# An early-fusion embedding kernel: GpSimd's products of the graph edges go to VectorE, with four node numbers packed in a register

## The reference, cut to what matters

```python
def _gat(x, src, dst, W, a_s, a_d, bias):
    h = (x @ W).reshape(G, Jn, H, C)
    es = jnp.einsum('gjhc,hc->gjh', h, a_s)[:, src]
    ed = jnp.einsum('gjhc,hc->gjh', h, a_d)[:, dst]
    e = jax.nn.leaky_relu(es + ed, 0.2)
    ...
    w = jnp.exp(e - m[:, dst])
    den = jnp.zeros((G, Jn, H), e.dtype).at[:, dst].add(w)
    alpha = w / den[:, dst]
    out = jnp.zeros((G, Jn, H, C), e.dtype).at[:, dst].add(alpha[..., None] * h[:, src])
    return out.reshape(G, Jn, H * C) + bias
```

## Time and profile before

| what | us |
|---|---|
| device time, median of 3 runs (lowest to highest) | 6471.19 (6469.46 to 6471.34) |
| the profiled execution | 6495.84 |
| its span | 6494.1 |
| VectorE busy in the span | 5697.2 |
| GpSimd busy | 4760.5 |
| TensorE busy (matmuls) | 3920.4 |
| ScalarE busy | 3243.8 |

### The profile page before, as it was taken

How to read it: one execution, slowest core, us unless ns; L and a number is a source line. 1 busy time by engine, 2 the same in 40 slices (tenths; PEclk the granted TensorE clock), 3 DMA queues, 4 the chain that set the end, 5 groups by cost and what they waited for, 6 DMA issues and landing times. The chain is left out here.

```text
span 6494.1 us, 61166 instructions
## 1 busy us (share of the span) xinstructions
PE 3920.4 (60%) x13720; PEld 2254.6 (35%) x13720; DVE 5697.2 (88%) x7312; ACT 3243.8 (50%) x5534; POOL 4760.5 (73%) x3337
## 2 busy tenths in 40 slices
PE   3213412215676776776767767767667676667777
PEld 3102411213343333333433333334333333245556
DVE  3677666765999999999999999999999999967778
ACT  1112211214566656666666666666566665544445
POOL 4362145225999999999999999999999999833334
PEclk9656556657999999999999999999999999987878
DMA  1000000003444444444444444444444444300000
GB/s 26 1 1 11 2 1 1 11 18 116 160 163 168 160 166 165 160 174 160 165 165 160 166 164 161 173 160 165 165 160 166 164 160 170 141 4 2 2 2 2
DMA packets 171496, 695.04 MB, mean 107 GB/s; under 512 B 27970, under 2 KB 34627, under 8 KB 171139
## 3 DMA queue, kind: packets, MB, share of 16 engines
q1 hardware_dynamic: 169608, 688.25, 29.6%
q0 software_dynamic: 1536, 3.14, 0.2%
HBM read 684.77 MB, written 6.55 MB: 106 GB/s over the span
## 5 line engine op out<-in xcount | busy, mean ns | idle before, releaser
L1022 PE MATMUL m_PS<-m_pr,ident 128*128 128x512 f32 (+1 forms) x6144 | 2496.3, 544 | 907.3 <-DVE m_pr L1146 907.1
L806 POOL TENSOR_TENSOR m_hs<-m_u,m_BC 128x1280 f32<-128x1280 f32 x1024 | 2975.9, 2906 | 68.6 <-DVE m_u L1163 68.6
L1138 DVE TENSOR_TENSOR_SCAN m_hs<-m_PS,m_hs 128x640 f32<-128x640 f32 x2048 | 2934.8, 1467 | 5.2 <-POOL m_hs L806 3.0
L863 ACT ACTIVATE m_PS<-m_dt,m_A 128x640 f32<-128x640 f32 x2048 | 1613.3, 794 | 909.9 <-DVE m_hs L1138 896.3
L1022 PEld LDWEIGHTS m_PS<-m_pr,ident 128*128 128x128 f32 x6144 | 1134.9, 195 | 2167.8 <-DVE m_pr L1146 1133.1
L813 POOL TENSOR_TENSOR m_pr<-m_hs,m_BC 128x384 f32<-128x384 f32 x1024 | 1070.1, 1045 | 184.5 <-DVE m_hs L1138 179.9
L1146 DVE TENSOR_TENSOR m_pr<-m_hs,m_PS 128x896 f32<-128x896 f32 x1024 | 1079.8, 1055 | 8.2 <-DVE m_hs L1138 8.0
L270 POOL TENSOR_TENSOR g_prod<-g_hbuf,g_E 128x128 f32<-128x128 f32 (+1 forms) x888 | 471.1, 548 | 832.7 <-ACT g_E L320 636.3
L852 ACT COPY m_PS<-m_BC 128x448 f32<-128x448 f32 x1024 | 546.5, 534 | 155.8 <-DVE m_pr L1146 107.5
L354 PE MATMUL g_TB<-ident,g_nrm 128*128 128x128 f32 x200 | 66.2, 332 | 574.7 <-DVE g_nrm L490 569.9
L557 DVE TENSOR_TENSOR g_accA<-g_accA,g_prod 128x128 f32 x592 | 255.2, 431 | 158.0 <-DVE g_accA L557 122.1
(11 more groups left out here) (241 smaller groups left out, 4435.8 us busy)
## 6 DMA issues: line engine op xcount, KB each, us to landing
m_BC<-m_scr SPq DMA_DIRECT2D x1024, 640.0 KB, 3.8
m_scr<-m_CB SPq DMA_DIRECT2D x32, 160.0 KB, 4.2
m_hs<-in_cwr SPq DMA_DIRECT2D x4, 512.0 KB, 3.9
out<-f_res SPq DMA_DIRECT2D x20, 64.0 KB, 1.5
m_inw<-in_in_w SPq DMA_DIRECT2D x4, 256.0 KB, 4.0
m_dtw<-in_dw SPq DMA_DIRECT2D x4, 256.0 KB, 3.6
m_xw<-in_xw SPq DMA_DIRECT2D x8, 64.0 KB, 3.8
m_outw<-in_ow SPq DMA_DIRECT2D x4, 128.0 KB, 3.4
```

What stands on the lines that cost most here:

```text
L806: pool.tensor_tensor(hs[:, g % RH], u[:, p % 2], BC[:, g % UB:g % UB + 1, 0:S].to_broadcast([P, DT, S]), ALU.mult).then_inc(w_ready, 1)
L863: act.activation(half[d], dt_[:, p % 2, d], ACT.Exp, scale=A[:, l, d, n:n + 1]).then_inc(da_ready, 1)
L1022: ins = pe.matmul(Y[:, a:e], ident[:], pr[:, g % RP, a:e], start=False, stop=False, skip_group_check=True)
L1138: v.tensor_tensor_scan(hs[:, g % RH, d, :], half[d], hs[:, g % RH, d, :], 0.0, ALU.mult, ALU.add).then_inc(scan_done, 1)
```

## The change

GpSimd's whole edge loop is taken out, with its registers and loads. VectorE now makes the product of edge `e` and then adds the product of edge `e - 1`, in turn, through the same ring of four buffers. The four numbers of two neighbouring edges (source and destination of each) go into one word of 4 x 6 bits, so the 74 words now serve both sides and VectorE's loads stay as many as they were. `node` takes the side as well, and needs a shift, a mask or both. The wait for the last addition sits on the addition instruction itself, instead of on a semaphore instruction in front of it. The setup has one more packing step.

```diff
--- before.py
+++ after.py
@@ -36,14 +36,14 @@
     NR, XR = 4, 4
     LAG_P, LAG_T = 2, 3
     RING = 4
-    SHIFT = 4096
+    BITS = 6
     NPK = NE // 2
     KEEP = 48
     LOAD = 26
     E1, E2 = P, NE - P
     KEY = 256.0
     LOW = -3.0e38
-    assert J % 2 == 0 and NE % 2 == 0 and NPK < 2 * KEEP and P < NE <= KEY and 2 * J <= P
+    assert J % 2 == 0 and NE % 2 == 0 and NPK < 2 * KEEP and P < NE <= KEY and J <= 1 << BITS and 2 * J <= P
 
     with ExitStack() as ctx:
         def sb(name, shape, dt=F32):
@@ -94,7 +94,8 @@
         srt = sb("srt", [P, 2, NE])
         nodes = at(Ef, 6 * NE, 2, NE)[0:1]
         pack = at(M, 7 * P, 2, NPK)[0:1]
-        pack_i = sb("pack_i", [1, 2, NPK], I32)
+        word = at(F, 0, NPK)[0:1]
+        pack_i = sb("pack_i", [1, NPK], I32)
         hot = sb("hot", [P, 2, NE])
         keepf = sb("keepf", [P, H, NE])
         resetf = sb("resetf", [P, H, NE])
@@ -169,21 +170,22 @@
 
             eng.sem_inc(waits_met, 1)
 
-        def load(eng, regs, side, first, last):
+        def load(eng, regs, first, last):
 
             for a in range(first, last, LOAD):
                 w = min(LOAD, last - a)
                 at = a - first
-                eng.load(regs[at:at + w], pack_i[0:1, side, a:a + w])
-
-        def node(eng, reg, regs, e):
-
-            packed = regs[e // 2 % KEEP]
-            if e % 2:
-                eng.reg_alu(reg, packed, 12, ALU.logical_shift_right)
-            else:
-                eng.reg_alu(reg, packed, SHIFT - 1, ALU.bitwise_and)
-            return nc.s_assert_within(eng.snap(reg, min_val=0, max_val=SHIFT - 1), 0, J - 1,
+                eng.load(regs[at:at + w], pack_i[0:1, a:a + w])
+
+        def node(eng, reg, regs, e, side):
+
+            packed, lift = regs[e // 2 % KEEP], (e % 2 * 2 + side) * BITS
+            if lift:
+                eng.reg_alu(reg, packed, lift, ALU.logical_shift_right)
+                packed = reg
+            if lift < 3 * BITS:
+                eng.reg_alu(reg, packed, (1 << BITS) - 1, ALU.bitwise_and)
+            return nc.s_assert_within(eng.snap(reg, min_val=0, max_val=(1 << BITS) - 1), 0, J - 1,
                                       skip_runtime_bounds_check_because="the numbers are clamped to J - 1 before they are packed")
 
         def in_turn(*steps):
@@ -251,27 +253,6 @@
                                                 in_offset=bass.IndirectOffsetOnAxis(ap=ids[:, k, n:n + 1], axis=0),
                                                 bounds_check=3 * VOCAB - 1, oob_is_err=False
                                                 ).then_inc(rows_loaded, 16)
-                src = [pool.alloc_register(f"g_src{q}") for q in range(KEEP)]
-                here = pool.alloc_register("g_here")
-                pool.wait_ge(set_dve, 1)
-                load(pool, src, 0, 0, KEEP)
-                for pb in range(PB):
-                    for l in range(3):
-                        lp = pb * 3 + l
-                        C = COUT[l] // H
-                        if lp:
-                            load(pool, src, 0, 0, NPK - KEEP)
-                        pool.wait_ge(sm_act, lp * N_SA + N_SA)
-                        for e in range(NE):
-                            if e == 2 * KEEP:
-                                load(pool, src, 0, KEEP, NPK)
-                            j = node(pool, here, src, e)
-                            pool.wait_ge(added, lp * NE + e + 1)
-                            pool.tensor_tensor(
-                                prod[:, e % RING, :, 0:COUT[l]].rearrange("p b (h c) -> p b h c", c=C),
-                                hb[l][:, :, bass.ds(j, 1), :].rearrange("p b o (h c) -> p b (o h) c", c=C),
-                                E[:, :, :, e:e + 1].to_broadcast([P, 2, H, C]),
-                                ALU.mult).then_inc(prod_ready, 1)
 
             @block.scalar
             def _(act):
@@ -436,8 +417,9 @@
                 chain(v.tensor_scalar(hot[:, 1, :], srt[:, 1, :], iota_p[:, 1:2], None, ALU.is_equal))
                 chain(v.tensor_tensor(hot[:, 0, :], hot[:, 0, :], hot[:, 1, :], ALU.add))
                 chain(v.tensor_scalar(nodes[:], srt[0:1], float(J - 1), 0.0, ALU.min, ALU.max))
-                chain(v.scalar_tensor_tensor(pack[:], nodes[:, :, 1:NE:2], float(SHIFT), nodes[:, :, 0:NE:2], ALU.mult, ALU.add))
-                chain(v.tensor_copy(pack_i[:], pack[:]))
+                chain(v.scalar_tensor_tensor(pack[:], nodes[:, :, 1:NE:2], float(1 << 2 * BITS), nodes[:, :, 0:NE:2], ALU.mult, ALU.add))
+                chain(v.scalar_tensor_tensor(word[:], pack[:, 1, :], float(1 << BITS), pack[:, 0, :], ALU.mult, ALU.add))
+                chain(v.tensor_copy(pack_i[:], word[:]))
                 chain(v.memset(keepf[:], 0.0))
                 chain(v.memset(keepr[:], 0.0))
                 same = [srt[:, 1, 1:NE].unsqueeze(1).to_broadcast([P, H, NE - 1]),
@@ -465,7 +447,7 @@
                 v.wait_ge(set_dve, 1)
 
                 dst = [v.alloc_register(f"g_dst{q}") for q in range(KEEP)]
-                there = v.alloc_register("g_there")
+                here, there = v.alloc_register("g_here"), v.alloc_register("g_there")
                 keepf_f = keepf[:].rearrange("p h e -> p (h e)")
                 resetf_f = resetf[:].rearrange("p h e -> p (h e)")
                 keepr_f = keepr[:].rearrange("p h e -> p (h e)")
@@ -511,9 +493,9 @@
                         lp = pb * 3 + l
                         D0 = lp * N_SM
                         if lp:
-                            load(v, dst, 1, 0, NPK - KEEP)
+                            load(v, dst, 0, NPK - KEEP)
                         else:
-                            load(v, dst, 1, 0, KEEP)
+                            load(v, dst, 0, KEEP)
                         for bb in range(2):
                             v.wait_ge(sm_act, lp * N_SA + 3 + bb)
                             v.tensor_tensor(E[:, bb].rearrange("p (a h) e -> p a (h e)", a=2),
@@ -546,15 +528,28 @@
                             v.wait_ge(sm_act, lp * N_SA + 7 + bb)
                             v.tensor_tensor(E2d[:, bb], E2d[:, bb], F2[:, bb], ALU.subtract).then_inc(sm_dve, 1)
 
+                        C = n // H
                         av = acc[l][:].rearrange("p (b j) c -> p b j c", b=2)
-                        for e in range(NE):
-                            if e == 2 * KEEP:
-                                load(v, dst, 1, KEEP, NPK)
-                            j = node(v, there, dst, e)
-                            v.wait_ge(prod_ready, lp * NE + e + 1)
-                            v.wait_ge(added, lp * NE + e + RING)
-                            to = av[:, :, bass.ds(j, 1), :].rearrange("p b o c -> p b (o c)")
-                            v.tensor_tensor(to, to, prod[:, e % RING, :, 0:n], ALU.add).then_inc(added, 1)
+                        v.wait_ge(sm_act, lp * N_SA + N_SA)
+                        for e in range(NE + 1):
+                            if e < NE:
+                                if e == 2 * KEEP:
+                                    load(v, dst, KEEP, NPK)
+                                j = node(v, here, dst, e, 0)
+                                v.wait_ge(added, lp * NE + max(e + 1 - RING, 0) + RING)
+                                v.tensor_tensor(prod[:, e % RING, :, 0:n].rearrange("p b (h c) -> p b h c", c=C),
+                                                hb[l][:, :, bass.ds(j, 1), :].rearrange("p b o (h c) -> p b (o h) c", c=C),
+                                                E[:, :, :, e:e + 1].to_broadcast([P, 2, H, C]),
+                                                ALU.mult).then_inc(prod_ready, 1)
+                            if e:
+                                i = e - 1
+                                v.wait_ge(prod_ready, lp * NE + i + 1)
+                                to = av[:, :, bass.ds(i_at, 1), :].rearrange("p b o c -> p b (o c)")
+                                ins = v.tensor_tensor(to, to, prod[:, i % RING, :, 0:n], ALU.add)
+                                ins._wait_ge(added, lp * NE + i + RING)
+                                ins.then_inc(added, 1)
+                            if e < NE:
+                                i_at = node(v, there, dst, e, 1)
                         v.wait_ge(added, lp * NE + NE + RING)
 
                         for nd in range(2 * J):
```

## The result

| | before | with the change |
|---|---|---|
| device time, median (lowest to highest) | 6470.32 us (6468.07 to 6471.34) | 6389.45 us (6386.78 to 6391.48) |
| ratio, 95% interval | | 0.9875 (0.9858 to 0.9892) |

The change makes the kernel 80.9 us faster, 1.25%.

What follows compares the result with a forecast made beforehand. It took a chain of additions inside VectorE, lengthened by GpSimd's reads, as the bound. Layers 0 and 2 (+13.4 us), layer 1 (-53.8) and packing (+0.2) gave -40.2 us from 6471.19: 6431 us, range 6395 to 6480.

Steps and rivals of the forecast that it cites:

- The bound before: Edge loops before: each VectorE addition waits until the last is written; GpSimd's reads beside it lengthen this by 0.23 us.
- The load of 26 registers in mid-loop: VectorE's register load inside each edge loop: claimed to stay at 5.8 us of queue time.
- The queue's price: VectorE's instruction queue in layers 0 and 2: 736 and 568 ns at even and odd edges, 0.652 us on average.
- hand-over: Gap between instructions in VectorE's queue: 0.044 us each, the two engine instructions counting 44 ns together.
- Pauses: VectorE's queue stands still about 0.35 us after each 128 instructions: 0.022 us more per edge.
- Layer 1: Queue and engine nearly tie: 0.69 us per edge, 107.9 us a loop against 134.80, twice -26.9 us.
- Rival 2: Engine bound at full durations in layer 1, 0.848 us per edge: 6478 us, no change; chance 0.11.
- Rival 1: VectorE's queue stands still while an instruction waits for the engine, in all edge loops: 6526 us, slower; chance 0.09.
- Rival 3: Queue cheap, the additions' own chain stays: 0.52 us per edge in layers 0 and 2, 6336 us; chance 0.06.
- The sum by its own steps: Whole kernel: layers 0 and 2 +13.4 us, layer 1 -53.8, extra packing step +0.2; together -40.2 us.
- Layer-0 loops of about 105 us, longer than now: Sign expected in the profile after: layer-0 loops at 105.6 us against 102.25 before.

Runs made afterwards that it cites:

- b_embed_only: The kernel before with one edit: VectorE's wait for its last addition sits on the addition itself, GpSimd still making the products; 6294.7 us, ratio 0.9731.
- a_shift: The changed kernel with its packed words 8 bytes further into their tile; 6423.4 us.
- a_wait: The changed kernel with the addition's wait put back into a semaphore instruction of its own in front of it; 6458.5 us.
- a_donate: The changed kernel with each cut number used from its own register instead of a copy, so fewer queue instructions; 6308.6 us, ratio to before 0.9751.
- hybrid: Products on GpSimd in layers 0 and 2, on VectorE in layer 1; wait on the addition, no register copies, all loads 16-byte aligned; 6239.3 us, ratio to before 0.9640.
- b_align: The kernel before with 76 words of room per side instead of 74, so VectorE's words start 304 bytes into the tile; 6435.6 us, ratio 0.9948.
- b_embed: The kernel before with the wider room for the words and the wait on the addition itself, GpSimd still making the products; 6268.9 us, ratio 0.9692.

## Why the prediction was right or wrong, point by point

- **The bound before**, a chain inside VectorE: right, shown by `b_embed_only`, which shortens nothing but that chain. The 0.77 us read for layer 1 was its period only up to edge 96; behind it is 1.08. The sum used the whole window of 134.80 us and so was not touched. The prediction did not draw the conclusion that the chain can be shortened with the products left where they were.
- **The step that failed** is "The load of 26 registers in mid-loop, 5.8 us of queue time, was on VectorE before and stays." The load stays, its duration does not: 2.07 us. I had read only the median of VectorE's row, beside whose 5.8 us its least of 1836 ns (22 registers) stood unused, and not GpSimd's. GpSimd's row of the same line, in the profile before, by single line:

```profile
L177 POOLq TENSOR_LOAD <-g_pack_i x13: 1999/2005/4924, 76.3 to 1336.5; - x13
```

  The load of 26 registers takes 2.0 us from the other side of the tile, which should have been asked about. It is worth 22.4 us in the loops and 11.6 between them, where the prediction had counted no change at all: 34.0 of the 40.7 us by which the sum was short. The other 6.6 are the loops of layers 0 and 2, together 7.3 shorter than forecast with slow loads, less 0.7 in layer 1.
- **The queue's price** in layers 0 and 2, 0.652 us: 0.640 measured, turns of 0.695 (0.736 forecast) and 0.584 (0.568). The hand-over is smaller between plain register operations than the 0.044 us taken from the idle time before: the queue's durations in an even turn are 45 + 2 x 40 + 77 + 36 + 2 x 57 = 352 ns, which leave 343 for nine instructions, 0.038 each. Luck has a part in this: the forecast had eight hand-overs of 0.044 in that turn, the two engine instructions counting half each, and nine of 0.038 come to about the same. The fused pair of the even turn takes 77 ns instead of 114, and the lone shift 45, near the 40 taken. With the load at its old price (`a_shift`) these loops take 103.8 on average against 105.6: -7.3 us over four.
- **Pauses**: 99.93 - 2.2 leaves 0.660 us an edge on average where the turns give 0.640, so 0.020 us against 0.022 forecast. In the first loop's trace the queue stands still nine times, about 0.35 us longer than otherwise, after each 128 recorded instructions (129 where the load lies between). If these are the crossings of blocks that the Trainium skill calls "mostly hidden" ("Runtime: NRT & Kernel Launch", Instruction fetch mechanics), that does not hold in this loop, where the 0.020 us times 592 edges are 12 us in full view; no run here shows that they are.
- **Layer 1**, 0.69 us an edge and 107.9 a loop: 108.3 in `a_shift`. Products and additions overlap as the pair before the loop did, 0.33 us from start to start. Rival 2 falls: the full 0.42 us are never paid. The Trainium skill ("VectorE: DVE Perf Modes", The DRAIN you can't avoid), which rival 2 drew on, says both that the next operation does not start until the pipe is empty and that one which is not held starts earlier. These starts, 0.08 us before the recorded end of the one in front, speak against full durations.
- **Rival 1**, the queue held by a waiting instruction: false for an instruction that waits at the engine. In a loop of layer 1 with the change the shift that stands behind an addition in the program starts at 380.66 us and that addition at 380.86, in layer 0 the pair is at 160.31 and 160.34. What does hold the queue is a wait in a semaphore instruction of its own (`a_wait`). **Rival 3**, a cheap queue: false as `a_wait` and `a_donate` show.
- The sum by its own steps, -40.2, less 6.6 for the edges and 34.0 for the loads, is -80.8; measured -80.9, closer than the interval of the ratio can vouch for.
- "Layer-0 loops of about 105 us, longer than now" is wrong by the loads alone: 103.8 with slow ones, 99.9 with fast.

## What to carry to other kernels

Before an instruction is carried over "as it was", compare its duration with every other instance of the same kind in the profile; where two differ by a factor for the same amount of work, something that the edit touches (here the byte at which a tile's part begins) may set it. Where one instruction of a chain waits on the last, put the wait on that instruction and leave address computations and other queue work ahead of it. And when a change moves work and edits a wait at the same time, try the edit of the wait by itself first: here it was worth twice the whole (-173.4 us in `b_embed_only` against -80.9).

## What the runs showed of the hardware

- A load of registers from SBUF costs about 0.08 us a register if it starts at a multiple of 16 bytes in the tile and 0.22 if not. On VectorE 26 registers took 2.07 and 5.8 us, 22 took 1.84 and 4.95; 20 from a good start took 1.36 (`hybrid`). On GpSimd 26 took 2.0 from a good start and 22 took 4.92 from a bad one. Starts at 4, 8 and 12 bytes beyond a multiple of 16 were all slow, and VectorE's load was fast with GpSimd reading the same tile (`b_align`) and slow without (`a_shift`).
- Each register instruction of VectorE's queue costs its duration and about 0.038 us. A semaphore instruction (21 ns) adds 0.07 in all. A fused pair with a shift takes 0.11 to 0.12 us, a shift by itself 0.045.
- A wait in a semaphore instruction holds VectorE's queue (0.08 us in the longer turn of `a_wait` in layer 1); an engine instruction that waits does not (with the change, a queue instruction at 380.66 us, the waiting addition in front of it at 380.86).
- Two engines that work beside each other do not simply add their times: a product of 128 numbers alone on GpSimd needs 0.37 us (four in 1.52 us from 212.75 us of the profile before, each taking 0.41), an addition on VectorE starts 0.21 behind its product when both are made there, and the two engines run together at 0.42 an edge in `b_embed`, while with VectorE's chain late by one semaphore and one address they settle at 0.73.
